# Two fused layers on one core: the inverse of the triangles on packed 32x32 diagonal squares instead of whole 128x128 tiles

## What is computed

```python
def step(W, qkv):                       # the recurrence of layer 1
    q_t, k_t, v_t = qkv
    y_t  = einsum('bds,bs->bd', W, q_t)
    pred = einsum('bds,bs->bd', W, k_t)
    W = W - 0.01 * (pred - v_t)[:, :, None] * k_t[:, None, :]
    return W, y_t
x = x + attention(layernorm(x)) * silu(experts(layernorm(x)))
x = x + recurrence(layernorm(x)) * silu(layernorm(x) @ sign(weight).T)
```

## Time and profile of the kernel before

| what | us |
|---|---|
| median of the runs | 754.84 |
| profiled execution, its own time | 758.75 |
| span of that execution | 756.9 |
| an iteration in the steady part | 79.9 |
| TensorE busy | 652.3 (86%) |
| VectorE busy | 445.2 (59%) |
| ScalarE busy | 360.2 (48%) |
| GpSimd busy | 236.8 (31%) |

### The profile page before, as it was taken

How to read it: one execution, slowest core, us unless ns; L and a number is a source line. 1 busy time by engine, 2 the same in 40 slices (tenths; PEclk the granted TensorE clock), 3 DMA queues, 4 the chain that set the end, 5 groups by cost and what they waited for, 6 DMA issues and landing times.

```text
span 756.9 us, 14228 instructions
## 1 busy us (share of the span) xinstructions
PE 652.3 (86%) x5606; PEld 452.7 (60%) x5606; DVE 445.2 (59%) x1015; ACT 360.2 (48%) x680; POOL 236.8 (31%) x358
## 2 busy tenths in 40 slices
PE   4167698979999899989998999899989998896874
PEld 2034365447766676657665866576757775555763
DVE  5566457555857676676748675858575755225331
ACT  3502435754557445644566455645564546561210
POOL 5703101223433153124404341423332403125331
PEclk9999989979999999999999999999999999998995
DMA  2732620360035102520053004500350000000000
GB/s 69 135 70 43 133 60 8 90 106 7 6 82 102 35 2 65 93 68 1 29 107 83 8 8 105 105 7 9 93 96 17 1 7 16 21 1 1 0 15 14
DMA packets 31378, 36.32 MB, mean 48 GB/s; under 512 B 4433, under 2 KB 26608, under 8 KB 31312
## 3 DMA queue, kind: packets, MB, share of 16 engines
q1 hardware_dynamic: 31312, 35.42, 21.8%
HBM read 24.46 MB, written 9.96 MB: 45 GB/s over the span
## 4 chain that ended last, share of the span: by engine, by line
PE 61%; DVE 15%; ACT 6%; issue 6%; DMA 6%; POOL 4%; SPq 2%; POOLq 0%; DVEq 0%; ACTq 0%
PE ps_v L838 7%; PE ps_s L817 7%; PE ps_e L802 6%; DMA kst<-split_scratch 4%; DVE cand L1285 4%; PE ps_a L764 4%; PE ps_e L799 4%; PE ps_c L907 4%; PE ps_c L920 3%; PE ps_a L752 3%; PE ps_a L727 3%; DVE second L1230 2%; PE ps_s L821 2%; DVE xn L1230 2%; PE ps_c L924 2%
## 5 line engine op out<-in xcount | busy, mean ns | idle before, releaser
L1285 DVE TENSOR_REDUCE cand<-ps_s 128x4 f32<-128x512 f32 (+1 forms) x320 | 212.8, 682 | 89.1 <-PE ps_s L821 69.1
L1087 ACT ACTIVATE prob<-ps_e 128x512 f32<-128x512 f32 x320 | 188.1, 596 | 150.9 <-PE ps_e L802 149.2
L817 PE MATMUL ps_s<-kst,qst 96*128 96x128 bf16 (+1 forms) x1024 | 134.4, 249 | 40.7 <-DMA kst<-split_scratch 22.9
L817 PEld LDWEIGHTS ps_s<-kst,qst 96*128 96x128 bf16 x1024 | 82.2, 105 | 98.2 <-issue 50.1
L802 PE MATMUL ps_e<-qst,kst 128*128 128x384 bf16 (+3 forms) x512 | 124.5, 305 | 0.0
L799 PE MATMUL ps_e<-identb,negmask 128*128 128x256 bf16 (+1 forms) x320 | 83.2, 260 | 8.1 <-ACT prob L1087 8.1
L838 PE MATMUL ps_v<-prob,vaug 128*32 128x512 f32 (+3 forms) x1024 | 88.6, 441 | 0.0
L638 POOL TENSOR_TENSOR second<-second,upmask 128x512 f32<-128x512 f32 x42 | 53.0, 1269 | 31.9 <-PE ps_c L907 31.9
L802 PEld LDWEIGHTS ps_e<-qst,kst 128*128 128x128 bf16 x512 | 50.6, 99 | 5.8 <-issue 0.6
L601 POOL CAST mparts<-nm 128x32 bf16<-128x32 f32 x16 | 3.4, 210 | 151.7 <-DVE nm L1292 151.7
L907 PE MATMUL ps_c<-second 128*128 128x128 f32 x336 | 47.2, 285 | 1.2 <-POOL second L638 0.7
(11 more groups left out here) (304 smaller groups left out, 1045.2 us busy)
## 6 DMA issues: line engine op xcount, KB each, us to landing
qst<-split_scratch SPq DMA_DIRECT2D x48, 192.0 KB
kst<-split_scratch SPq DMA_DIRECT2D x144, 64.0 KB
split_scratch<-qparts SPq DMA_DIRECT2D x8, 384.0 KB, 2.5
split_scratch<-kparts SPq DMA_DIRECT2D x8, 384.0 KB, 2.5
xn<-in_L_attn_x_dram SPq DMA_DIRECT2D x8, 256.0 KB, 3.1
x_res<-in_L_attn_x_dram SPq DMA_DIRECT2D x8, 256.0 KB, 6.8
out_dram<-second SPq DMA_DIRECT2D x7, 256.0 KB, 2.4
max_scratch<-mrow SPq DMA_DIRECT2D x16, 96.0 KB, 1.7
```

Of the source, the lines that this page charges most:

```text
L817: last = mm(ps_s[:, bank, w * n:w * (n + 1)], q[0:MAXROW, hd, tok(i)], k[0:MAXROW, hd, keys[0]:keys[1]], start=(n == 0), stop=True, skip_g ...
L1087: af(prob[:, u, :], ps_e[:, u % 2, :], ACT.Exp).then_inc(S["e_emptied"], 1)
L1285: vec.tensor_reduce(cand[:, i, h0:h0 + FILLS * (len(hds) - 1) + 1:FILLS, S_SLOT[u]], ps_s[:, u % 2, :].rearrange("p (a c) -> p a c", a=len ...
```

## The change

`inv`, `invT` and the products are no longer kept as whole 128x128 matrices up to level 4. The diagonal 32x32 squares of the four chunks are packed into [128, 4, 32] (`diag`, `inv_sq`, `invT_sq`, `a_sq`), and each product of a level is one of 32x32: four squares times four chunks, each in the tile of the array that its rows and its output have. Level 5 uses 32x32 tiles too, off the diagonal; level 6 uses 64x64. ScalarE now multiplies G by 0.01 and cuts the four squares out (four instructions on 32 partitions, ahead of the whole), GpSimd makes all masked squares at once in `c_gram` and nothing at the levels, and the squares are moved into the whole matrices by four ScalarE copies (`invT`) and two VectorE copies (`inv_lo`) after level 4. `left_minus` is gone, the zeroing of `ablk` too.

```diff
@@ GpSimd
             def c_gram(b):
-                g.memset(r.ablk[:, :, :], 0.0).then_inc(r.S["inv1_ready"], 1)
-                pool.wait_ge(r.S["c0_emptied"], o.count(C0_FILLS, C0_GRAM + 1))
-                g.tensor_tensor(r.sy[:, :, :], r.gram[:, :, :], bcast(lowmask0[:, :], 1, NT), ALU.mult)
-                g.tensor_tensor(r.inv[:, :, :], eye, r.sy[:, :, :], ALU.subtract)
-                pairs(b, 1)
-                pairs(b, 2)
-            def pairs(b, lv):
-                    if lv > 2:
-                        pool.wait_ge(r.S["c0_filled"], o.count(C0_FILLS, c0_a(lv - 2) + 1))
-                    g.tensor_tensor(r.pair_up[lv % 2][:, :, :], r.gram[:, :, :], bcast(upmask[:, lv, :], 1, NT), ALU.mult)
+                pool.wait_ge(r.S["diag_ready"], o.count(P // SQ, P // SQ))
+                g.tensor_tensor(r.a_sq, r.diag, bcast(low_sq[:, :], 1, NT), ALU.mult)
+                g.tensor_tensor(r.inv_sq, bcast(eye_sq[:, :], 1, NT), r.a_sq, ALU.subtract)
+                g.tensor_tensor(r.pair_up[:, 0, :, :], r.diag, bcast(up_sq[:, 0, :], 1, NT), ALU.mult)
+                g.tensor_tensor(r.pair_up[:, 1:, :, :], bcast(r.diag, 1, more), bcast(up_sq[:, 1:, :], 2, NT), ALU.mult)
@@ TensorE
+            def squares(bank, lhsT, rhs, at):
+                for i in range(NT):
+                    for row, col in at:
+                        last = mm(bank[SQ * col:SQ * col + SQ, SQ * i:SQ * i + SQ], lhsT(row, col, i), rhs[SQ * row:SQ * row + SQ, i, :],
+                                  start=True, stop=True, skip_group_check=True)
             def lev_a(b, lv):
-                for i in range(NT):
-                    last = mm(r.ps_c0[:, tok(i)], r.pair_up[lv % 2][:, i, :], r.inv[:, i, :], start=True, stop=True)
+                if lv <= IN_SQUARE:
+                    last = squares(r.ps_c0, of_squares(r.pair_up[:, lv - 1, :, :]), r.inv_sq, DIAG)
+                elif lv == IN_SQUARE + 1:
+                    last = squares(r.ps_c0, lambda row, col, i: r.gram[...], r.inv_sq, [(0, 1), (2, 3)])
+                else:
+                    pe.wait_ge(r.S["blocks_ready"], blocks_moved(b))
+                    for i in range(NT):
+                        last = mm(r.ps_c0[H:P, H * i:H * i + H], r.gram[0:H, i, H:P], r.inv_lo[0:H, i, :], start=True, stop=True,
+                                  skip_group_check=True)
             def lev_d(b, lv):
+                if lv <= IN_SQUARE:
+                    squares(r.ps_c0, of_squares(r.invT_sq), r.a_sq, DIAG).then_inc(r.S["c0_filled"], 1)
+                elif lv == IN_SQUARE + 1:
+                    squares(r.ps_c0, of_squares(r.invT_sq), r.a_sq, [(1, 1)]).then_inc(r.S["c0_filled"], 1)
+                    squares(r.ps_c1, of_squares(r.a_sq), r.invT_sq, [(1, 0), (3, 2)]).then_inc(r.S["c1_filled"], 1)
+                else:
+                    for i in range(NT):
+                        last = mm(r.ps_c1[0:H, H * i:H * i + H], r.a_hi[H:P, i, :], r.invT[H:P, i, H:P], ...)
@@ ScalarE
             def c_gram(b):
-                copy(r.gram[:, :, :].rearrange("p i d -> p (i d)"), r.ps_c0[:, :])
+                for n in range(P // SQ):
+                    nc.scalar.mul(r.diag[sq, :, :], r.ps_c0[sq, :].rearrange("p (i d) -> p i d", i=NT)[:, :, sq], LR)
+                nc.scalar.mul(r.gram[:, :, :].rearrange("p i d -> p (i d)"), r.ps_c0[:, :], LR)
             def lev_a(b, lv):
-                copy(half(r.ablk, lv, 0), half_bank(r.ps_c0, lv, 0))
+                    copy(r.a_sq, r.ps_c0[:, 0:P].rearrange("p (i c) -> p i c", c=SQ))
+            def lev_d(b):
+                act.wait_ge(r.S["invt_ready"], o.count(IN_SQUARE + 2, IN_SQUARE + 1))
+                for n in range(P // SQ):
+                    copy(r.invT[sq, :, sq], r.invT_sq[sq, :, :]).then_inc(r.S["blocks_ready"], 1)
+            pieces[f"lev_d{IN_SQUARE}"] = lev_d
@@ VectorE
             def lev_d(b, lv):
+                if lv <= IN_SQUARE:
+                    vec.tensor_tensor(r.inv_sq, r.inv_sq, bank(r.ps_c0, slice(0, P), SQ), ALU.subtract)
+                    squares_turned(r)
+                    if lv == IN_SQUARE:
+                        for n in range(2):
+                            vec.tensor_copy(r.inv_lo[sq, :, sq], r.inv_sq[sq, :, :]).then_inc(r.S["blocks_ready"], 1)
+                elif lv == IN_SQUARE + 1:
+                    vec.tensor_scalar(r.inv_lo[rows, :, 0:SQ], bank(r.ps_c0, rows, SQ), -1.0, None, ALU.mult)
+                    vec.tensor_scalar(r.invT[rows, :, SQ:2 * SQ], bank(r.ps_c1, rows, SQ), -1.0, None, ALU.mult)
+                    vec.tensor_scalar(r.invT[rows, :, H + SQ:P], bank(r.ps_c1, rows, SQ), -1.0, None, ALU.mult)
+                else:
+                    vec.tensor_scalar(r.invT[0:H, :, H:P], bank(r.ps_c1, slice(0, H), H), -1.0, None, ALU.mult)
```

More of the change, by code:

```diff
@@ L44 @@
 LEVELS = 7
+SQ = 32
+IN_SQUARE = 4
 A_FILLS = 17
@@ L54 @@
 C1_HT, C1_QT, C1_VK, C1_KQ, C1_FFN, C1_Y = 0, 1, 2, 3, 4, 7
-IN_SQUARE = 4
 def c0_a(k):
@@ L557, in masks @@
                                           pattern=[[2 * w, nb], [0, w]], channel_multiplier=-1))
+                for n in range(P // SQ):
+                    sq = slice(SQ * n, SQ * n + SQ)
+                    chain(g.tensor_copy(up_sq[sq, :, :], full[sq, :, sq]))
+                chain(g.memset(body.invT, 0.0))
+                chain(g.memset(body.inv_lo, 0.0))
                 pool.sem_inc(S["masks_ready"], 1)
@@ L648, in c_out, with zero_state @@
                 g.tensor_tensor(r.out_sb[:, :, :], x1[b.parity][:, :, :], r.syg[:, :, :], ALU.add).then_inc(r.S["out_ready"], 1)
-            levels = {f"lev_d{lv}": lambda b, lv=lv: pairs(b, lv + 2) for lv in range(1, LEVELS)}
-            run(pool, levels | {"ln1_norm": lambda b: ln_rstd(0, b), "ln2_norm": lambda b: ln_rstd(1, b), "ln3_norm": lambda b: ln_rstd(2, b),
+            def zero_state(b):
+                pool.wait_ge(S["e_filled"], b.count(GROUPS * UNITS, 0))
+                g.memset(last.state, 0.0)
+                g.memset(last.invT, 0.0)
+                g.memset(last.inv_lo, 0.0).then_inc(last.S["blocks_ready"], 1)
+            run(pool, {"ln1_norm": lambda b: ln_rstd(0, b), "ln2_norm": lambda b: ln_rstd(1, b), "ln3_norm": lambda b: ln_rstd(2, b),
                        "q": lambda b: split_rest(0, b), "k": lambda b: split_rest(1, b), "xnt": token_norms, "gates": gates,
                        "m_parts0": lambda b: m_parts(b, 0), "m_parts1": lambda b: m_parts(b, 1), "x1": x1_piece, "c_gram": c_gram, "c_out": c_out,
-                       "zero_state": lambda b: g.memset(last.state, 0.0)}, lambda *a: None, masks)
+                       "zero_state": zero_state}, lambda *a: None, masks)
         @block.tensor
@@ L897, in c_gram, with of_squares @@
                 last.then_inc(r.S["c1_filled"], 1)
+            def squares(bank, lhsT, rhs, at):
[3 more added lines that the diff above has]
+                                  start=True, stop=True, skip_group_check=True)
+                return last
+            def of_squares(t):
+                return lambda row, col, i: t[SQ * row:SQ * row + SQ, i, :]
+            DIAG = [(n, n) for n in range(P // SQ)]
+            H = 2 * SQ
             def lev_a(b, lv):
@@ L902, in lev_a, with blocks_moved @@
                 c0_fill(b, c0_a(lv))
-                pe.wait_ge(r.S["pair_ready"], o.count(LEVELS - 1, lv))
-                if lv == 1:
-                    pe.wait_ge(r.S["inv1_ready"], o.count(2, 2))
-                for i in range(NT):
-                    last = mm(r.ps_c0[:, tok(i)], r.pair_up[lv % 2][:, i, :], r.inv[:, i, :], start=True, stop=True)
+                if lv <= IN_SQUARE:
+                    pe.wait_ge(r.S["pair_ready"], o.count(2, min(lv, 2)))
+                    if lv == 1:
+                        pe.wait_ge(r.S["inv1_ready"], o.count(1, 1))
+                    last = squares(r.ps_c0, of_squares(r.pair_up[:, lv - 1, :, :]), r.inv_sq, DIAG)
+                elif lv == IN_SQUARE + 1:
+                    last = squares(r.ps_c0, lambda row, col, i: r.gram[SQ * row:SQ * row + SQ, i, SQ * col:SQ * col + SQ], r.inv_sq,
+                                   [(0, 1), (2, 3)])
+                else:
[3 more added lines that the diff above has]
+                                  skip_group_check=True)
                 last.then_inc(r.S["c0_filled"], 1)
+            def blocks_moved(b):
+                r, o = second_layer(b)
+                return o.count(6, 6) + (1 if b.c == SEQS - 1 else 0)
             def lev_d(b, lv):
@@ L1117, in c_gram @@
                 c0_full(b, C0_GRAM)
-                copy(r.gram[:, :, :].rearrange("p i d -> p (i d)"), r.ps_c0[:, :]).then_inc(r.S["c0_emptied"], 1)
+                for n in range(P // SQ):
+                    sq = slice(SQ * n, SQ * n + SQ)
+                    nc.scalar.mul(r.diag[sq, :, :], r.ps_c0[sq, :].rearrange("p (i d) -> p i d", i=NT)[:, :, sq], LR).then_inc(r.S["diag_ready"], 1)
```

(15 more changed lines are left out.)

101 lines of the change are left out of this document (54 added, 47 removed).

## The result

The changed kernel takes **719.15 us** (median of four runs, 718.63 to 720.81), the kernel before beside it 755.35. The ratio is 0.951, 95% interval 0.949 to 0.954. So 36.2 us are saved, where 44.5 were forecast; the range, 692 to 760, holds the time. The profiled execution has a span of 716.9 us.

A forecast was written before the change was run, and what follows sets the result against it. TensorE's list was taken to set the pace of a 79.9 us iteration, except in one stretch and the tail. Six iterations at 5.7 us (34) plus 10.5 in the tail, 44.5 off 754.84, gave 710.3 us; range 692 to 760.

The forecast's parts named there:

- TensorE's sum: TensorE's level products in an iteration: 11.6 us now, 5.3 after, so 6.3 us saved.
- the unknown on which the sum hung: Level products on TensorE: whether tiles on different rows of the array work at once; four at once taken.
- The change of shape: TensorE's list: 0.10 us for each change of tile shape, each way, 1.9 us an iteration.
- The stretch: 8.4 us per iteration, chain over VectorE and GpSimd: 1.45 us saved there in place of 1.4 of TensorE's, idle time unchanged.
- The new wait: Slot (2,6), behind `lev_d4`: ScalarE stops until VectorE has turned the squares; 0.7 us an iteration, bounds 0 and 2.
- An iteration: Iterations 2 to 7: 5.7 us saved in each, to 74.2 us; times six, 34 us.
- The tail: Behind the iterations, where each level waits for the one before: 13.7 us saved less 3.2 for the clock, 10.5 us.
- The 3.2 us put down for the clock: Tail: more gaps can spread the low granted clock; an eight-record piece takes 0.9 us longer, three or four such.
- B: Level squares don't run side by side, on different rows and writing one bank: 28 ns a record, 740 us; chance 0.18.
- C: TensorE's records: load and product come no faster than pairs now, 55 to 71 ns; 775 or 805 us; chance 0.14.
- D: Steady iterations: short records let the clock fall in half the levels' window, 8 us more each, about 790; chance 0.04.
- A: Whole kernel, the forecast itself: four tiles at once, 710 us, 696 to 724 by its bounds; chance 0.60.

The follow-up runs named there:

- the loop order: Changed kernel with the two loops of `squares` swapped, so the four chunks of one square follow each other on one tile: 738.24 us, ratio 0.975.
- the doubled products: Changed kernel with every 32x32 product of `squares` issued twice, 64 records in a piece of levels 1 to 4: 747.03 us, ratio 0.987.
- The late copies: Changed kernel with VectorE's two and ScalarE's four block copies moved from slot (2,6) to (2,8): 712.70 us, ratio 0.942.
- the one product: Changed kernel issuing only the first product of each call of `squares`, so the inverse is not computed: 712.67 us, ratio 0.943.
- the kernel before with half of its products: Kernel before with only two of the four chunks in each product of levels 1 to 6: 733.76 us, ratio 0.969.

## Why the prediction was right, and where it was off

- **TensorE's sum.** 6.3 us forecast, 5.7 measured. A piece of levels 1 to 4 takes 0.39 us (0.42 forecast) to the next one's start. The tiles side by side, the unknown on which the sum hung, are shown by the loop order (23 ns on one tile) and the doubled products (9.1 ns on four). The record was mis-sized: 28 / 4 = 7 ns taken, 9.1 measured, which over 256 records is 0.54 us, all but 0.1 of the difference. The price of one tile was too high (28 for 23), and four side by side don't give four times that (23 / 9.1 = 2.5). The change of shape fits: 0.10 us in a piece don't depend on the count. That they are its way out is inferred from the forecast, no run separates the two.
- **The stretch.** Normalizations -0.94 (forecast -0.95), transpose 0.31 (0.3), subtraction 0.28 (0.29), idle time 0.97 against 1.11 (no change). Right, and that GpSimd was the cause of the first is shown by putting its work back.
- **The new wait.** 0.7 us taken, 1.03 measured, and the step named the wrong engine. ScalarE's copies were priced with a wait; VectorE's two were put into a sum of VectorE time ("adds two block copies and small writes"), as if idle time covered them. In the profile they stand between the transpose of level 4 and a maximum for which TensorE waits, beside L585 of GpSimd, which holds one of them for its whole length. The order of VectorE's list at (2,6) and what GpSimd does there were both to be had from the trace of before. The late copies show it: 1.2 us an iteration for both.
- **A cover that was not named.** The wait at the gates grew from 0.29 to 0.75 us because the piece that hid it shrank. I asked what hides the added work, not what the removed work had been hiding. That is 0.46 us. The kernels with pieces of other lengths bear it out. At the same place, one tile has a piece of 0.83 us (to the next piece's start) and a wait of 0.32, the doubled products 0.68 and 0.45, the one product 0.17 and 0.96. The first and the last of these waits:

```profile
345.98 0.39 PE L824 MATMUL ps_s<-kst,qst 96*128 96x256 bf16 x2 [0.32 <-DVE cand L1335]
```

```profile
337.34 0.39 PE L824 MATMUL ps_s<-kst,qst 96*128 96x256 bf16 x2 [0.96 <-DVE cand L1335]
```

Piece and wait together are 1.13 to 1.15 us each time, as with 0.38 + 0.75 after the change: what the piece loses, the wait gains.

- **An iteration:** 5.7 forecast; 5.7 of records + 0.14 - 1.03 - 0.46 gives 4.4, and the chain says 4.5. Times six it is 27 and not 34: that is 7 of the 8.3 us missed. So TensorE's sum was near, and the term that was too small is what comes back as waits: 0.7 us forecast, 1.03 + 0.46 measured.
- **GpSimd** 8.1 us less (forecast 10.7 - 2.4 = 8.3), **VectorE** 2.1 less (2 or so).
- **The tail,** 10.5 forecast, 10.1 measured. That the sum is so near is luck, as its terms are off both ways. Levels 1 to 4 of sequence 7: -4.8 (-5.4). Levels 5 and 6: -0.6 (-1.3). Levels of sequence 6 with the layer norms beside them: 26.0 to 19.1, -6.9 (-5, between 3 and 8). Ahead of level 1: +0.8 (-2.0). TensorE's wait of 1.13 us for GpSimd at its end is gone, but the stage ran at a granted clock of 0.80, where it was 1.00, and has 10.0 us of TensorE's records in 10.6: two pieces of two records of 512 columns (L879, L884), at 0.52, take 3.4 us where they took 1.7. The 3.2 us put down for the clock have the right sign, but their place is here and in the levels of sequence 6 (0.66, where it was 0.87), not in levels 1 to 4 of sequence 7, which ran at 1.00. Levels 5 and 6 ran at 0.66, where it was 1.00: a piece of level 6 takes 1.1 us there and 0.68 in an iteration, which is about what the two levels miss. The whole cost of the clock was not measured by itself. Up to the first level of sequence 6 the tail is 1.0 longer (47.0 to 48.0), which has no term in the prediction and stays open.
- **The rivals.** B (the tiles of different rows don't run together when they write one bank) falls: all sixteen products of a piece write the bank `ps_c0` and come at 9.1 ns a record. The rule of the Trainium skill beside it (TensorEngine Tiling (Array Packing), Gotcha 1: PSUM Pressure) is not borne out here for 32x32 tiles that also differ in their columns; row tiles over the same columns were not run. C falls by the doubled products. D: the clock stayed at 1.00 in the iterations, with 312 short records in each. It does fall behind a wait of 1.99 us in the kernel before with half of its products; that is a fall behind a wait, and no run shows one by short records. For A the prediction gives 696 to 724; its two bounds, of the new wait and of the levels of sequence 6, give only 703 to 720 when added up. The measured 719 lies in both, near the dear end.

The iteration that the prediction names as its sign, 74.2 us, is near that of the kernel with both copies late (74.3), but not for its reasons: there the 0.7 us put down for the new wait are not spent, and the dearer record and the wait at the gates take their place. Two things were missing in the mechanism: where two small copies stand, and what the removed products had covered.

## What to carry to other kernels

When work is taken off the engine that sets the pace, list for each removed piece whose wait it was covering: a piece of 1.0 us that shrinks to 0.4 opens the chain behind it. Small added operations are costed by the place in their engine's list, not by their sum: ask who waits for the next instruction there and what GpSimd does at that time. And where two causes hold the same place, removing one can show little because the second takes over, so move both before judging either.

## What the runs showed that I had not expected

- 32x32 float32 records follow each other every 9.1 ns on four diagonal tiles in one bank, and every 23 ns on one tile; the order of two loops is worth 18 us. The Trainium skill (TensorE: Matmul & The Clock Gate, section "Wait — 56ns, not 53.3ns?") has a start-to-start that "never drops below ≈25 ns however small N is". The one-tile rows, at 23, are near it; with four tiles the rows, at 9.1, are far below.
- One VectorE operation between buffers in SBUF beside a GpSimd product of 1.15 us took 1210 ns where the other took 290. In the tail both copies of sequence 7 are long, 957 and 1309 ns, and two GpSimd products of 1.26 us stand beside them. The maxima, which read PSUM, kept 0.6 to 0.7 us beside the same product once the copies were gone (1.25 for two, in the kernels with late copies).
- The end of the kernel runs at half the clock, 0.50 for 21 us. Dummy products behind the last pieces alone give 4.9 us of the tail back in the traces, spread over the whole tail 3.3.
